# Sums of key blocks on GpSimd for two of four head groups, and norms, halves and first scores at other slots of a hand-written order

## The chip, the cores and the metric

The kernel runs on one core of a Trainium2 chip. A core has five engines with a queue of instructions each: PE (TensorE, matrix products; its weight loads are shown apart as PEld), DVE (VectorE), ACT (ScalarE), POOL (GpSimd) and SP (SyncE, which here issues most DMAs). Each queue is worked in order. Engines wait for one another by semaphores. The metric is the device time in microseconds (us) of one execution; lower is better.

## The reference

One transformer block, 16 sequences of 512 tokens with 512 features, 16 heads of 32, then a mixture of 32 experts (4 for each token) and a shared expert:

```python
x = x + attention(layernorm(x))
x = x + moe(layernorm(x))
# attention, for each sequence and head:
scores = einsum('bsnh,btnh->bnst', k, q) / sqrt(32)
scores = triu(scores) + -10000.0 * tril(ones, k=-1)
attn = softmax(scores, axis=2)
out = einsum('bnkq,bknh->bqnh', attn, v) @ Wo + bo
```

The softmax runs over the keys. Its denominator for a query is the sum of exp(scores) over the keys that are not masked.

## The kernel before

Two parts run one after the other: the sequences (attention, router and shared expert) and then the 32 experts. The change touches the first part alone.

The sequences are worked in 18 turns. Turn i does the projections of sequence i, the attention of sequence i - 1, and the output projection, router and shared expert of sequence i - 2. Turns 0, 1 and 2 and turns 15, 16 and 17 lack some of these; turns 3 to 14 stand in a loop of two turns at a time. A turn has 126 slots (`N_SLOTS`). Each engine walks through the same slots in its own function `turn`, and at each slot issues what the tables at the top of the file (`ST_SLOT`, `S_SLOT` and so on) put there. So the order of each queue is written out by hand, and the tables are the only thing that sets it. A dense product of the projections or the shared expert takes one to four slots on PE. A slot of it is three fp16 matmuls (L172, L173, L174), since each operand is held as a high and a low half.

Heads are worked in four groups of four (`QUARTER`, at slots 0, 30, 60 and 90). For a group, and counted from its first slot:

- PE makes the scores with queries in the partitions (`scores`, L524) in ten fills, f = 0 to 9, of two banks in turn, at the slots of `S_AT`. DVE takes their maxima (`maxima`, L917) one slot later; PE may write fill f only when the maxima of fill f - 2 are read. The first group (0) is that of the next sequence, and its fills lie at slots 85 to 111. `NM_SLOT` follows the last fill by two slots: the maxima are transposed there, and SP places them for the exponentials.
- PE makes the transposed scores, keys in the partitions (`scores_T`, L539), in ten fills at slots 0, 2, ... 18. ACT takes the exponential one slot later (`exp`, L650) and writes `probs`, 1280 columns of f32 for each head: for key block 0 its 512 queries, for the blocks 1, 2 and 3 the 384, 256 and 128 that are not masked (`PCOL` says where each block starts).
- POOL zeroes the triangles on the diagonal (`triangles`, L1033), for two heads each at slots 11 and 20.
- PE forms the product with V (`values`, L548 into `o_ps`) at slot 23 and the product of a matrix of ones with `probs` (`denominators`, L548 into `scores_T`) at slot 25. The latter gives the denominators in f32, 16 matmuls with 32 columns of weights each, the four heads in four column groups of the array.
- DVE transposes and inverts the denominators at slot 26 (`reciprocals`, L931 to L935), normalises at slot 30 (`normalise`, L939), ACT takes the high half at slot 31 (`att_hi`, L656), DVE the low half at slot 35 (`att_lo`, L943).

The other work that the steps below speak of: the statistics of the next sequence are on DVE at slots 82, 84, 86 and 88 (`statistics1`, L697), their scales on POOL two slots later (`scales1`, L1001 to L1006), the norms on ACT at slots 87 to 93 (`norm1`, L628), and the transposes on PE at slots 106, 107, 112 and 113 (L481). The router's selection is a chain of small DVE steps, one at each slot from 73 to 93. The GLU of the shared expert is on ACT (L622) and DVE (L894, L899). From turn 3 on POOL issues one of 16 scatters of router records (L1042) at each third slot from 61 to 106. POOL also subtracts for the low halves of q and k (`qk_lo`, L1025) and adds the output bias to the residual (L1019).

In the trace of a steady turn, slots are recognised by these operations: the product with V of the third group is slot 83, fill 0 of the first scores is slot 85, and the transposed scores f = 3 of the fourth group are slot 96.

Of the kernel before, what the change touches and what calls it, by code (L numbers as in the profile page):

```python
# [11 lines left out]
ALU = mybir.AluOpType  # L12
# [3 lines left out]
P = 128  # L16
BATCH, SEQ, D = 16, 512, 512
# [54 lines left out]
def last_slot(kind, n):  # L72
    at = 0
    for k, m, pieces in GROUPS:
# [5 lines left out]

QUARTER = (0, 30, 60, 90)
FILLS = 10
ST_SLOT = {base + 2 * f: (q, f) for q, base in enumerate(QUARTER) for f in range(FILLS)}

S_AT = {1: range(1, 21, 2), 2: (23, 25, *range(31, 47, 2)), 3: (47, 49, 51, 53, *range(61, 73, 2)),
        0: (85, 91, 94, 97, 100, 103, 105, 107, 109, 111)}
S_SLOT = {slot: (hg, f) for hg, slots in S_AT.items() for f, slot in enumerate(slots)}
EXP_SLOT = {slot + 1: at for slot, at in ST_SLOT.items()}
MAX_SLOT = {slot + 1: at for slot, at in S_SLOT.items()}
NM_SLOT = {slot + 2: hg for slot, (hg, f) in S_SLOT.items() if f == FILLS - 1}  # L90
TRI_SLOT = {base + at: (q, p) for q, base in enumerate(QUARTER) for p, at in enumerate((11, 20))}
PV_SLOT = {base + 23: q for q, base in enumerate(QUARTER)}
DEN_SLOT = {base + 25: q for q, base in enumerate(QUARTER)}
RDEN_SLOT = {base + 26: q for q, base in enumerate(QUARTER)}
ATT_SLOT = {base + 30: q for q, base in enumerate(QUARTER)}
AHI_SLOT = {base + 31: q for q, base in enumerate(QUARTER)}
ALO_SLOT = {base + 35: q for q, base in enumerate(QUARTER)}

S_FILL = tuple(piece for p in range(2) for piece in (
    ((2 * p, 3, 0, 512),), ((2 * p, 0, 0, 128), (2 * p, 2, 128, 384)),  # L100
# [9 lines left out]

LN2_SLOT = {last_slot("out", t) + 4: t for t in range(TT)}
STAT_SLOT = {slot: t for t, slot in enumerate((82, 84, 86, 88))}
LN1_SLOT = {slot + 5: t for slot, t in STAT_SLOT.items()}

ROUTE_FROM = last_slot("router", 0) + 1
DEST_FROM = [last_slot("pos", n) for n in range(2)]
# [170 lines left out]
def sequences(nc, a, c, ps):  # L287
    with ExitStack() as ctx:
# [19 lines left out]

        s_done, s_read, nm_ready = sem("s_done"), sem("s_read"), sem("nm_ready")
        nm_placed = [sem("nm_placed0"), sem("nm_placed1")]  # L310
        st_done, exp_done, tri_done = sem("st_done"), sem("exp_done"), sem("tri_done")
        den_done, den_read, o_done, att_done = sem("den_done"), sem("den_read"), sem("o_done"), sem("att_done")
        aT_hi, aT_ready = sem("aT_hi"), sem("aT_ready")

# [145 lines left out]
        def _(pe):  # L460
# [82 lines left out]
            def columns(bank, loaded):  # L543

                for kt in range(TT):
                    for h in range(GH):
                        n = SEQ - kt * P
                        last = pe.matmul(bank[h * HD:(h + 1) * HD, kt * P:SEQ], loaded(kt, h),  # L548
                                         c["probs"][:, h, PCOL[kt]:PCOL[kt] + n], start=kt == 0, stop=kt == TT - 1)
                return last  # L550

            def denominators(s, hg):

                n = s * HG + hg
                pe.wait_ge(tri_done, (n + 1) * 2)
                pe.wait_ge(exp_done, (n + 1) * FILLS)
                columns(ps["scores_T"][1], lambda kt, h: c["ones"][:, 0:HD]).then_inc(den_done, 1)

            def values(s, par, hg):
                n = s * HG + hg  # L560
# [437 lines left out]
        def _(pool):  # L998
# [28 lines left out]
            def triangles(s, hg, p):  # L1027

                pool.wait_ge(exp_done, (s * HG + hg) * FILLS + (p + 1) * FILLS // 2)
                settle(pool)  # L1030
                for kt in range(TT):
                    blk = c["probs"][:, 2 * p:2 * p + 2, PCOL[kt]:PCOL[kt] + P]
                    last = pool.affine_select(out=blk, in_=blk, compare_op=ALU.is_ge, fill=0.0, base=0,  # L1033
                                              pattern=[[0, 2], [1, P]], channel_multiplier=-1)
                last.then_inc(tri_done, 1)

            def scatter(s, n):
                t, k = divmod(n, TOPK)
                if n == 0:
                    pool.wait_ge(dest_ready, s + 1)  # L1040
                    settle(pool)
                pool.indirect_dma_start(  # L1042
                    out=a["slots"], out_offset=bass.IndirectOffsetOnAxis(ap=c["idx"][:, t, k:k + 1], axis=0),
                    in_=c["rec"][:, t, k, :], in_offset=None, bounds_check=SLOTS - 1,
                    oob_is_err=False).then_inc(slots_scattered, 16)

            def turn(i, par, proj, attn, fin, nxt):
                for slot in range(N_SLOTS):
                    if attn and slot in TRI_SLOT:
                        triangles(i - 1, *TRI_SLOT[slot])  # L1050
                    if proj and slot in QLO_SLOT:
                        qk_lo(i, *QLO_SLOT[slot])
                    if fin and slot in BIAS_SLOT:
                        add_bias(i - 2, BIAS_SLOT[slot])
                    if fin and slot in SCALE2_SLOT:
                        scales2(i - 2, SCALE2_SLOT[slot])
                    if nxt and slot in SCALE1_SLOT:
                        scales1(i + 1, SCALE1_SLOT[slot])
                    if (not isinstance(i, int) or i > 2) and slot in SCATTER_SLOT:
                        scatter(i - 3, SCATTER_SLOT[slot])  # L1060
# [255 lines left out]
def transformer_block(nc, a):  # L1316
    with ExitStack() as ctx:
# [6 lines left out]
        with ExitStack() as first:  # L1324
            def sb(name, shape, dt=F32):
                return first.enter_context(nc.sbuf_tensor(name, shape, dt))
# [18 lines left out]
            c["glu"], c["att"], c["denT"] = sb("glu", [P, 2, 512]), sb("att", [P, SEQ]), sb("denT", [P, SEQ])  # L1345
            c["junk"] = sb("junk", [P, 2, SEQ], F16)
            c["nmax"], c["nmF"], c["nmT"] = sb("nmax", [P, 32]), sb("nmF", [P, 32]), sb("nmT", [P, 2, 32], F16)
            c["rden"] = sb("rden", [P, SEQ // 32])
            c["bqk"] = sb("bqk", [P, 2 * HG])
            c["bvT"], c["bo"], c["maskrow"] = sb("bvT", [P, DK]), sb("bo", [P, D]), sb("maskrow", [P, SEQ], BF16)  # L1350
# [76 lines left out]
```

## Time and profile before

| what | value |
|---|---|
| median of 3 runs | 2513.14 us (2513.05 to 2518.89) |
| profiled execution | 2517.61 us, of which 2515.8 us span |
| mean granted PE clock | 0.966 of full speed |
| PE busy | 2311.3 us, 92% |
| DVE, ACT, POOL busy | 63%, 43%, 44% |
| from 2100 us on | the experts |

The page gives shares over the whole span; a timeline gives single instructions in the order of their start, with the idle time before them on their engine and what ended it.

### The profile page before, as it was taken

Reading aid. Unit: us, or ns where it says so; the run is one execution under the profiler, and the core shown is the slowest. Engines: PE = TensorE matmul, PEld = TensorE weight load, DVE = VectorE, ACT = ScalarE, POOL = GpSimd, SP = SyncE. Lnnn points to the kernel's source line nnn. Section 1 sums busy time; section 2 is a strip of 40 time slices with the busy share of each in tenths; the row PEclk is TensorE's granted clock in tenths of the full one; section 3 lists DMA queues with packets and bytes.
Section 4 is the critical chain, followed back from the end, with each engine's and each line's share of the span. In section 5 each row is a group of like instructions: output and inputs, shape, how many; then the busy total and the mean of one; then the engine's idle time right before and its main releaser. Section 6 shows DMA issues by size and latency. Waiting matters only on the chain. (4 is left out here: it accounts for less than half of the span.)

```text
span 2515.8 us, 48721 instructions
## 1 busy us (share of the span) xinstructions
PE 2311.3 (92%) x15466; PEld 1159.8 (46%) x15466; DVE 1573.3 (63%) x4870; ACT 1083.8 (43%) x1849; POOL 1110.4 (44%) x1622
## 2 busy tenths in 40 slices
PE   3789999999999999999999999999998985999997
PEld 1334444444444444444444444444443443666664
DVE  4355666675766666666666666666666564666664
ACT  3344444444343434343434443434443313666664
POOL 1223244434343434444444444444443354777775
PEclk8889999999999999999999999999998897999999
DMA  4212222222222222222222222222212016888886
GB/s 166 68 43 60 53 69 58 67 55 72 57 66 61 65 67 57 66 69 61 60 61 60 60 60 60 60 60 60 62 41 76 10 55 184 230 233 238 236 234 121
DMA packets 180850, 222.52 MB, mean 88 GB/s; under 512 B 37776, under 2 KB 119792, under 8 KB 180624
## 3 DMA queue, kind: packets, MB, share of 16 engines
q1 hardware_dynamic: 154000, 177.58, 23.7%
q0 software_dynamic: 26624, 42.12, 7.5%
q8 instruction: 118, 1.93, 0.3%
q14 instruction: 108, 0.88, 0.1%
HBM read 112.65 MB, written 56.46 MB: 67 GB/s over the span
## 5 line engine op out<-in xcount | busy, mean ns | idle before, releaser
L917 DVE CUSTOM_DVE_ANT_0 junk<-scores,maskrow 128x512 f16<-128x512 f32 (+3 forms) x1024 | 462.5, 487 | 198.2 <-PE scores L524 130.8
L650 ACT ACTIVATE probs<-scores_T 128x512 f32<-128x512 f32 x640 | 369.6, 598 | 215.8 <-PE scores_T L539 212.9
L1033 POOL TENSOR_SCALAR_AFFINE_SELECT probs<-probs 128x256 f32<-128x256 f32 x512 | 192.6, 413 | 380.8 <-ACT probs L650 379.9
L539 PE MATMUL scores_T<-stack_q,stack_k 97*128 97x512 f16 (+3 forms) x1024 | 251.9, 308 | 53.3 <-ACT probs L650 42.7
L1042 POOL DMA_INDIRECT slots_dram<-rec,idx x256 | 258.8, 1011 | 89.0 <-issue 80.1
L524 PE MATMUL scores<-stack_k,stack_q 96*128 96x512 f16 (+3 forms) x1024 | 253.7, 310 | 44.6 <-DVE nmax L917 41.0
L172 PE MATMUL dense<-xT_hi,wqkv_hi 128*128 128x512 f16 x512 | 196.1, 383 | 1.5 <-DVE xT_lo L888 1.5
L173 PE MATMUL dense<-xT_lo,wqkv_hi 128*128 128x512 f16 x512 | 195.0, 381 | 0.0
L174 PE MATMUL dense<-xT_hi,wqkv_lo 128*128 128x512 f16 x512 | 194.9, 381 | 0.0
L1019 POOL TENSOR_TENSOR xres<-xres,bo 128x512 f32<-128x512 f32 x64 | 81.2, 1268 | 247.3 <-DMA xres<-in_x 247.3
L1159 POOL DMA_INDIRECT out<-ex_y,ex_sidx x96 | 153.3, 1597 | 76.6 <-issue 39.1
L607 ACT ACTIVATE glu<-dense,bqk 128x512 f32<-128x512 f32 x128 | 88.0, 687 | 218.4 <-PE dense L174 211.8
L524 PEld LDWEIGHTS scores<-stack_k,stack_q 96*128 96x128 f16 x1024 | 95.4, 100 | 183.9 <-DVE nmax L917 93.1
L539 PEld LDWEIGHTS scores_T<-stack_q,stack_k 97*128 97x128 f16 x1024 | 98.6, 100 | 174.1 <-ACT probs L650 55.7
L1025 POOL TENSOR_TENSOR split_q<-glu,split_q 128x512 f16<-128x512 f32 x64 | 74.3, 1161 | 217.2 <-ACT split_q L607 217.2
L548 PE MATMUL o_ps<-probs,v 128*32 128x512 f32 (+3 forms) x2048 | 156.5, 447 | 8.1 <-POOL probs L1033 5.5
L548 PE MATMUL scores_T<-probs,ones 128*32 128x512 f32 (+3 forms) x2048 | 151.2, 436 | 0.0
L1137 POOL DMA_INDIRECT ex_xg<-x2n_dram,ex_gidx x96 | 118.6, 1235 | 47.1 <-POOL ex_gidx L1132 27.6
L888 DVE SCALAR_TENSOR_TENSOR xT_lo<-dense,xT_hi 128x512 f16<-128x512 f32 x128 | 87.9, 689 | 78.9 <-ACT xT_hi L598 78.9
L1001 POOL TENSOR_SCALAR mv<-mv 128x1 f32<-128x1 f32 x128 | 29.5, 231 | 230.4 <-DVE mv L699 226.7
L931 DVE STREAM_TRANSPOSE denT<-scores_T 128x512 f32<-128x512 f32 x64 | 45.8, 716 | 136.1 <-PE scores_T L548 136.1
L598 ACT ACTIVATE xT_hi<-dense 128x512 f16<-128x512 f32 x128 | 74.4, 598 | 106.9 <-PE dense L481 91.5
(229 smaller groups left out, 5486.2 us busy)
## 6 DMA issues: line engine op xcount, KB each, us to landing
stack_q<-split_q SPq DMA_DIRECT2D x384, 64.0 KB, 2.0
stack_k<-split_k SPq DMA_DIRECT2D x384, 64.0 KB, 2.3
out<-xres SPq DMA_DIRECT2D x67, 256.0 KB, 3.1
xres<-in_x SPq DMA_DIRECT2D x64, 256.0 KB, 2.9
x2n_dram<-x2n SPq DMA_DIRECT2D x16, 1024.0 KB
ex_raw_wg<-in_W_gate SPq DMA_DIRECT2D x32, 512.0 KB, 4.1
ex_raw_wu<-in_W_up SPq DMA_DIRECT2D x32, 512.0 KB, 5.1
ex_raw_wd<-in_W_down SPq DMA_DIRECT2D x32, 512.0 KB, 8.6
```

The source lines that it names most:

```text
L172: pe.matmul(out, w[0], x[0], start=start, stop=False)
L173: pe.matmul(out, w[0], x[1], start=False, stop=False)
L174: return pe.matmul(out, w[1], x[0], start=False, stop=stop)
L524: last = pe.matmul(bank[:, at:at + cols], c["stack_q"][0:SROWS, hg, h, qt * P:(qt + 1) * P], c["stack_k"][0:SROWS, hg, h, 0:cols], start=T ...
L539: last = pe.matmul(bank[:, at:at + cols], c["stack_k"][0:SROWS + 1, hg, h, kt * P:(kt + 1) * P], c["stack_q"][0:SROWS + 1, hg, h, kt * P:k ...
L548: last = pe.matmul(bank[h * HD:(h + 1) * HD, kt * P:SEQ], loaded(kt, h), c["probs"][:, h, PCOL[kt]:PCOL[kt] + n], start=kt == 0, stop=kt = ...
L650: act.activation(to, at, ACT.Exp, scale=SCALE / (QS * QS)).then_inc(exp_done, 1)
L917: last = dve.tensor_tensor_reduce(out=c["junk"][:, f % 2, at:at + cols], in0=ps["scores"][f % 2][:, at:at + cols], in1=c["maskrow"][:, SEQ ...
L1033: last = pool.affine_select(out=blk, in_=blk, compare_op=ALU.is_ge, fill=0.0, base=0, pattern=[[0, 2], [1, P]], channel_multiplier=-1)
L1042: pool.indirect_dma_start(out=a["slots"], out_offset=bass.IndirectOffsetOnAxis(ap=c["idx"][:, t, k:k + 1], axis=0), in_=c["rec"][:, t, k, ...
L1137: pool.indirect_dma_start(out=e_["xg"][q][0:r, ch, :], out_offset=None, in_=a["x2n"], in_offset=bass.IndirectOffsetOnAxis(ap=e_["gidx"][q] ...
L1159: pool.indirect_dma_start(out=a["out"], out_offset=bass.IndirectOffsetOnAxis(ap=e_["sidx"][q][0:r, ch:ch + 1], axis=0), in_=e_["y"][q][0:r ...
```

## The change

For the head groups 1 and 2 (slots 30 and 60) POOL adds the key blocks 1, 2 and 3 of `probs` into a new tile `psum` of 384 columns a head, in three adds for two heads each (768, 512 and 256 elements in a partition) directly behind the triangles of the same heads. For these groups the product with ones then has 128 columns of block 0 and 384 columns of `psum` a head, in 8 matmuls where there were 16, with a wait for the adds. It moves from slot 25 to 27 of its group, the reciprocals from 26 to 28. The groups 0 and 3 keep the old form.

In all groups the high half moves from slot 31 to 33 (group 3: from 121 to 122) and the low half from 35 to 36 (group 3: from 125 to 124). The norms of the next sequence move from slots 87, 89, 91 and 93 to 94, 96, 98 and 100. The fills of the first scores move as the first hunk shows.

```diff
+SUMMED = (1, 2)
-        0: (85, 91, 94, 97, 100, 103, 105, 107, 109, 111)}
+        0: (85, 91, 93, 96, 99, 101, 104, 107, 110, 113)}
-DEN_SLOT = {base + 25: q for q, base in enumerate(QUARTER)}
-RDEN_SLOT = {base + 26: q for q, base in enumerate(QUARTER)}
+DEN_SLOT = {base + 25 + 2 * (q in SUMMED): q for q, base in enumerate(QUARTER)}
+RDEN_SLOT = {base + 26 + 2 * (q in SUMMED): q for q, base in enumerate(QUARTER)}
-AHI_SLOT = {base + 31: q for q, base in enumerate(QUARTER)}
-ALO_SLOT = {base + 35: q for q, base in enumerate(QUARTER)}
+AHI_SLOT = {slot: q for q, slot in enumerate((33, 63, 93, 122))}
+ALO_SLOT = {slot: q for q, slot in enumerate((36, 66, 96, 124))}
-LN1_SLOT = {slot + 5: t for slot, t in STAT_SLOT.items()}
+LN1_SLOT = {slot + 12: t for slot, t in STAT_SLOT.items()}
@@ PE: denominators
-                columns(ps["scores_T"][1], lambda kt, h: c["ones"][:, 0:HD]).then_inc(den_done, 1)
+                if hg not in SUMMED:
+                    columns(ps["scores_T"][1], lambda kt, h: c["ones"][:, 0:HD]).then_inc(den_done, 1)
+                    return
+                pe.wait_ge(summed, (s * len(SUMMED) + SUMMED.index(hg) + 1) * 2 * 3)
+                for at, x in ((0, c["probs"][:, :, 0:P]), (P, c["psum"])):
+                    for h in range(GH):
+                        last = pe.matmul(ps["scores_T"][1][h * HD:(h + 1) * HD, at:at + x.shape[2]], c["ones"][:, 0:HD], x[:, h, :], start=True, stop=True)
+                last.then_inc(den_done, 1)
@@ POOL
+            def block_sums(s, hg, p):
+                n = (s * len(SUMMED) + SUMMED.index(hg)) * 2 + p
+                pool.wait_ge(tri_done, (s * HG + hg) * 2 + p + 1)
+                if p == 0:
+                    need(pool, den_done, s * HG + hg)
+                heads = slice(2 * p, 2 * p + 2)
+                to, of = c["psum"], c["probs"]
+                pool.tensor_tensor(to[:, heads, :], of[:, heads, P:SEQ], of[:, heads, PCOL[1]:PCOL[1] + 384], ALU.add).then_inc(summed, 1)
+                pool.wait_ge(summed, n * 3 + 1)
+                pool.tensor_tensor(to[:, heads, P:384], to[:, heads, P:384], of[:, heads, PCOL[2]:PCOL[2] + 256], ALU.add).then_inc(summed, 1)
+                pool.wait_ge(summed, n * 3 + 2)
+                pool.tensor_tensor(to[:, heads, 256:384], to[:, heads, 256:384], of[:, heads, PCOL[3]:PCOL[3] + P], ALU.add).then_inc(summed, 1)
@@ POOL: turn
                     if attn and slot in TRI_SLOT:
                         triangles(i - 1, *TRI_SLOT[slot])
+                        if TRI_SLOT[slot][0] in SUMMED:
+                            block_sums(i - 1, *TRI_SLOT[slot])
@@ memory
+            c["psum"] = sb("psum", [P, GH, SEQ - P])
```

## Rows read from the trace of the kernel before

**Rows 1.** Page, part 1: busy time of each engine, share of the span, instructions.
```profile
PE 2311.3 (92%) x15466; PEld 1159.8 (46%) x15466; DVE 1573.3 (63%) x4870; ACT 1083.8 (43%) x1849; POOL 1110.4 (44%) x1622
```
**Rows 2.** Timeline of PE, slots 83 to 100: start, duration, line, form, [idle before].
```profile
1014.57 2.36 PE L548 MATMUL o_ps<-probs,v 128*32 128x512 f32 x32
...
1018.17 0.38 PE L524 MATMUL scores<-stack_k,stack_q 96*128 96x512 f16 x1
...
1031.05 0.39 PE L539 MATMUL scores_T<-stack_q,stack_k 97*128 97x384 f16 x2 [2.52 <-ACT probs L650]
...
1032.63 0.63 PE L174 MATMUL dense<-xT_hi,suT_lo 128*128 128x512 f16 x1
...
1035.99 0.38 PE L539 MATMUL scores_T<-stack_q,stack_k 97*128 97x512 f16 x1
```
**Rows 3.** Timeline of PE, slot 96 two turns later.
```profile
1276.17 0.39 PE L539 MATMUL scores_T<-stack_q,stack_k 97*128 97x384 f16 x2 [2.52 <-ACT probs L650]
```
**Rows 4.** Waits of PE: who for whom, us in total, times, longest.
```profile
PE scores_T L539 <- ACT probs L650: 42.7, 22, 3.9
PE scores L524 <- DVE nmax L917: 41.0, 44, 3.9
```
**Rows 5.** Timeline of PE: slot 71 of one turn, slots 111 to 115 of another.
```profile
1128.86 0.39 PE L524 MATMUL scores<-stack_k,stack_q 96*128 96x256 f16 x2 [0.65 <-DVE nmax L917]
...
1045.84 0.39 PE L524 MATMUL scores<-stack_k,stack_q 96*128 96x256 f16 x2 [0.72 <-DVE nmax L917]
...
1050.78 2.36 PE L548 MATMUL scores_T<-probs,ones 128*32 128x512 f32 x32
1053.07 0.39 PE L172 MATMUL dense<-sdT_hi,hT_hi 128*128 128x512 f16 x1
```
**Rows 6.** Timeline of ACT, same turn as rows 2, slots 89 to 93.
```profile
1027.22 0.81 ACT L628 ACTIVATE x2n<-x2n,mv 128x512 f32<-128x512 f32 x1 [2.18 <-POOL mv L1006]
1029.39 0.63 ACT L656 ACTIVATE aT_hi<-att 128x512 f16<-128x512 f32 x1 [1.36 <-DVE att L939]
...
1030.40 0.59 ACT L650 ACTIVATE probs<-scores_T 128x512 f32<-128x512 f32 x1
```
**Rows 7.** Timeline of DVE, same turn, slots 84 to 92.
```profile
1019.00 0.69 DVE L894 SCALAR_TENSOR_TENSOR glu<-glu,dense 128x512 f32<-128x512 f32 x1 [2.48 <-ACT glu L622]
...
1023.64 0.69 DVE L917 CUSTOM_DVE_ANT_0 junk<-scores,maskrow 128x512 f16<-128x512 f32 x1 [0.37 <-DVE att L935]
...
1030.86 0.08 DVE L917 DVE_READ_ACCUMULATOR2_ANT nmax<- 128x1 f32 x1
```
**Rows 8.** Page, part 5: additions and subtractions of POOL, busy and mean ns.
```profile
L1019 POOL TENSOR_TENSOR xres<-xres,bo 128x512 f32<-128x512 f32 x64 | 81.2, 1268 | 247.3 <-DMA xres<-in_x 247.3
...
L1025 POOL TENSOR_TENSOR split_k<-glu,split_k 128x512 f16<-128x512 f32 x64 | 74.2, 1160 | 60.6 <-ACT split_k L607 60.6
```
**Rows 9.** Timeline of POOL, second head group, slot 50.
```profile
1109.26 1.49 POOL L1033 TENSOR_SCALAR_AFFINE_SELECT probs<-probs 128x256 f32<-128x256 f32 x4 [2.90 <-ACT probs L650]
```
**Rows 10.** Timeline of PE, second head group, slots 55 and 57.
```profile
1114.50 2.36 PE L548 MATMUL scores_T<-probs,ones 128*32 128x512 f32 x32
...
1118.10 0.60 PE L492 MATMUL dense<-ident,x2n 128*128 128x128 f32 x4
```
**Rows 11.** Timeline of POOL, same turn as rows 2, third head group, slots 71 to 80.
```profile
1006.05 1.49 POOL L1033 TENSOR_SCALAR_AFFINE_SELECT probs<-probs 128x256 f32<-128x256 f32 x4 [11.64 <-ACT probs L650]
1007.70 0.99 POOL L1042 DMA_INDIRECT slots_dram<-rec,idx  x1 [0.16 <-issue]
...
1010.27 0.97 POOL L1042 DMA_INDIRECT slots_dram<-rec,idx  x1 [0.30 <-issue]
1012.40 1.54 POOL L1033 TENSOR_SCALAR_AFFINE_SELECT probs<-probs 128x256 f32<-128x256 f32 x4 [1.15 <-ACT probs L650]
```
**Rows 12.** Timeline of PE, turn 1: two waits and what follows them.
```profile
168.46 4.05 PE L548 MATMUL o_ps<-probs,v 128*32 128x512 f32 x32 [2.34 <-POOL probs L1033]
...
178.37 0.39 PE L524 MATMUL scores<-stack_k,stack_q 96*128 96x512 f16 x1 [1.79 <-DVE nmax L917]
```

More of the change, by code:

```diff
@@ L310, in sequences @@
         nm_placed = [sem("nm_placed0"), sem("nm_placed1")]
-        st_done, exp_done, tri_done = sem("st_done"), sem("exp_done"), sem("tri_done")
+        st_done, exp_done, tri_done, summed = sem("st_done"), sem("exp_done"), sem("tri_done"), sem("summed")
         den_done, den_read, o_done, att_done = sem("den_done"), sem("den_read"), sem("o_done"), sem("att_done")
```

## Prediction

> **What bounds the kernel now.** I read the page's busy times first, then the waits of PE, then one sequence turn of PE's timeline and, beside it, what VectorE, ScalarE and GpSimd do in the same microseconds. PE is busy in 92% of the span [rows 1], so every stage is PE's unless a wait shows otherwise. The 126 slots of a turn are worked in about 122.6 us: the same wait stands at 1031.05 and at 1276.17, two turns later [rows 2, 3], and (1276.17 - 1031.05) / 2 = 122.6. In a steady turn PE waits three times: 0.65 us at slot 71 (1128.86), about 2.5 to 2.9 us at slot 96, and 0.72 us at slot 111 [rows 2, 4, 5]. The long wait costs more than its length. From 1.6 us after it, matmuls of 512 columns take 0.63 us instead of 0.38, and follow each other at 0.43 instead of 0.22, until 1035.99 [rows 2]: ten of them at 0.21 extra, some 1.65 us. So PE's own work is the bound in all of the turn but slots 84 to 97.
>
> That stretch has another bound behind it. ScalarE reaches the exp for which PE waits only at 1030.40, held first by a norm that waits for GpSimd, then by a high half that waits for VectorE [rows 6]. But VectorE is itself full: from 1019.00 (GLU of slot 84, 0.8 us after PE ended that slot at 1018.17) it works without a pause, bar 0.37 us, until the maxima of score fill 1 are read at 1030.94 [rows 2, 7]. That is 11.9 us of VectorE work per turn, and PE may not write score fill 3 before it is done. This is the point to hold on to: moving norms and halves takes ScalarE's wait away, not VectorE's.
>
> **The change, part by part.**
>
> Shorter product with ones. Today the 16 matmuls of one head group start at 1050.78 and the next work at 1053.07: 2.3 us for 1280 columns a head, four heads beside each other [rows 5]. The new form has 128 + 384 = 512 columns a head. By columns alone 2.3 x 512/1280 = 0.92 us; I add 0.1 for starting and take 1.0, so 1.3 us saved, for two of four groups in 16 turns. If it were all PE's bound, 32 x 1.3 = 42 us.
>
> The three adds on GpSimd. One call adds 2 x 384, 2 x 256 and 2 x 128 elements, 1536 together. The nearest row is the add of 512 f32 elements at 1268 ns [rows 8]. Whatever part of it is fixed, three adds with 512 elements in the mean cost 3 x 1.268 = 3.8 us; with two hand-overs, at the 0.16 us that lie between the triangles and the next work of this engine [rows 11], I take 4.1 us. The lower bound is 3 x 1.16 = 3.5 by the subtraction row [rows 8]; the upper is 4.6, with 0.2 us for each of three hand-overs and 5% on each add. Per turn there are four calls, 16 us, which GpSimd has idle in sum (it is busy 44% [rows 1]); only their place matters.
>
> The Trainium skill (GPSIMD Engine Reference, section 3.1) puts a two-input add at about 2.6 cycles an element at 1.2 GHz, and calls the engine the wrong choice for plain elementwise work. An estimate by that page is 1536 x 2.6 / 1.2 = 3.3 us before dispatch, where the row gives 3.8; by it the stall below would be 0.5 us shorter. The trace agrees within the dispatch that the page leaves open.
>
> Second head group (slots 30 to 59). Its second triangle call starts at 1109.26 and ends at 1110.75 [rows 9]; the adds then end at 1114.9. The product, moved from slot 55 to 57, comes 1.3 us (two slots) after 1114.50, at 1115.8 [rows 10]. So it does not wait, with 0.9 us to spare; even the upper bound of the adds, 0.5 us more, leaves 0.4. Behind the first call only a subtraction for k is late (1100.5 to 1104), read by nobody for several slots. The reciprocals follow two slots later and PE is not held by them. Gain 1.3 us a turn; the wait at slot 71 moves with PE and stays 0.65.
>
> Third head group (slots 60 to 89). Here GpSimd's queue matters. After the first triangle call (1006.05 to 1007.54) it issues three scatters of slots 73, 76 and 79, ending at 1011.24, idles 1.15 us, and runs the second call from 1012.40 to 1013.94; PE needs it for the product with V at 1014.57 [rows 2, 11]. The spare time is 1.15 + 0.63 = 1.8 us. The first call's adds are put in front of the three scatters: 4.1 - 1.8 = 2.3 us too late, so PE stalls 2.3 us at slot 83, where it never waited. Bounds: 3.5 - 1.8 = 1.7 and 4.6 - 1.8 = 2.8. A stall of 2.34 us in front of this same product was followed by 4.05 us for it instead of 2.36; after 1.79 us the next matmul took its 0.39 [rows 12]. So I add the 1.65 us at the lower clock: PE ends slot 84 by 4.0 us late. The second call's adds end near 1021.2, before PE comes to the product at slot 87 near 1024: no wait there.
>
> What is late next: the 11.9 us of VectorE begin with the GLU of slot 84 and no step among them is moved out before the maxima of slot 92 (reciprocals go from 86 to 88, the normalisation stays at 90). So score fill 3, now at slot 96, goes out at 1031.05 + 4.0. PE waits there again, longer than now (its own work from slot 84 to there is some 9 us), with the same loss of clock afterwards as today. The 1.3 us saved at slot 87 vanish in that wait. In exchange, one score fill (0.2 us) now lies before the wait's end instead of after it.
>
> Norms, high and low halves. The norms at slots 94 to 100 instead of 87 to 93, the high half at 93 instead of 91: ScalarE no longer stands before the exps of slots 91 and 93. Four norms and three exps around slots 94 to 100 are some 5.5 us in 7 us of PE work, which fits. The gain is nil because of VectorE. The transposes that need the norms are at 106 and later.
>
> First scores. The fills at 93, 96, 99, 101, 104, 107, 110, 113 leave VectorE more time at the end: the wait of 0.72 us at slot 111 [rows 5] should go, 0.7 us gained. The maxima are sent two slots later, but are needed at slot 0 of the next turn; I see some 3 us left there, so nothing.
>
> **The sum.** Per steady turn: -1.3 (second group) + 4.0 (stall and clock, carried on by VectorE) - 0.2 - 0.7 = +1.8 us. Scatters, and so this queue, are in turns 3 to 16; 13 of these (3 to 15) have all parts: 13 x 1.8 = +23 us. Turn 2 has no scatters: -2.2. Turn 1 has a stall at the same product already [rows 12], which gets some 2 to 3 us longer and is partly paid by the shorter products; turn 16 has no first scores and loses the stall of 4.0 less 2.6. I take the three together as nil, with 3 us to either side. The stage of the experts is untouched. The profiled execution is 2515.8 us of span and 1.8 around it, 2517.6, so it would become 2541; it lies 4.5 above the median of the runs, 2513.1, and against the median the forecast is 2536.
>
> **The rivals.**
>
> Rival 1, GpSimd is early enough (faster). If the adds cost 1.8 us or less per call, no stall arises at slot 83. Then VectorE still binds slot 96, and a turn gains 1.3 + 0.2 + 0.7 = 2.2 us: 14 x 2.2 = 31, about 2482. Against it: 1.8 us for 1536 elements would be twice the rate of [rows 8]. A smaller form of it: stall of 1.7 us without loss of clock ([rows 12] shows none after 1.79), so -1.3 + 1.7 - 0.9 = -0.5 a turn, 2507, within or just beyond what counts as no change.
>
> Rival 2, the stall comes but is absorbed (faster). If VectorE isn't the bound at slot 96 (because its work shrinks while PE stands, or ScalarE alone made the wait), then today's 2.7 + 1.65 us go, the 4.0 take their place, and both products gain: -1.3 - 1.3 - 0.7 - 0.3 = -3.6 a turn, 2463 to 2470. For it: the wait in [rows 2, 4] is put down to ScalarE. Against: VectorE's maxima end 0.11 us before PE resumes [rows 2, 7].
>
> Rival 3, the two stalls together cost more clock (slower). They stand some 14 us apart; if the second low stretch is twice as long, 1.65 us more a turn, or if the later maxima delay the residual loads and so GpSimd in the first group by 0.5 us: 13 x 2 = +26, about 2560.
>
> Rival 4, the change doesn't act: the stall and the gains cancel, 2513.
>
> **How the numbers follow.** Forecast 0.50; rival 1 full 0.12, its smaller form 0.10; rival 2 0.10; rival 3 0.14; rival 4 0.04. Three tenths of a per cent, 7.5 us, is what a measurement of this kernel can tell from no change. Faster: 0.12 (rival 1) + 0.10 (rival 2) + 0.03 of the smaller form = 0.25. Same: the rest of the small form, rival 4, and 0.02 of the forecast's low side = 0.13. Slower 0.62. The forecast's own range is 2524 to 2550 (stall 1.9 to 2.8). For 8 in 10 I go from 2475 to 2558; that leaves out rival 2 and part of rival 3. The cases of both signs lie in it.
>
> **What would show it.** Right: PE's product with V at slot 83 waits 2.3 us for the triangles of the third group; the second triangle call starts directly behind a scatter; score fill 3 waits for VectorE's maxima; the short products take 1.0 us; the wait at 111 is gone; a turn lasts 124.4 us. The three adds show 1.8, 1.27 and 0.7 us. Wrong: no wait at slot 83, or a wait at slot 96 that is gone while VectorE is idle there, or turns below 121 us.

## The result, and the profile after

The changed kernel takes 2551.82 us (median of 4 runs, 2549.71 to 2555.69) beside 2514.64 us for the kernel before in the same comparison: a ratio of 1.0147, interval 1.0128 to 1.0166. It is slower by 37 us, where 23 us were forecast (2536 us): inside the range given for 8 in 10 (2475 to 2558), just above the forecast's own range (2524 to 2550). Its profiled execution took 2550.47 us, 2548.7 of them span. That is 32.9 us of span more than before, and 32.4 of these lie in the twelve steady turns 3 to 14.

The page of after, part 1, answers to [rows 1]: GpSimd is busy 53% of the span, and TensorE is busy for fewer microseconds in a longer span, at the lower share of 90%.

```profile
PE 2292.3 (90%) x14954; PEld 1145.2 (45%) x14954; DVE 1604.5 (63%) x4870; ACT 1083.4 (43%) x1849; POOL 1357.0 (53%) x1814
```

The waits of PE in after (who for whom, us in total, times, longest), beside [rows 4]:

```profile
PE scores L526 <- DVE nmax L926: 82.1, 72, 3.5
PE o_ps L550 <- POOL probs L1042: 40.2, 22, 5.0
...
PE scores_T L541 <- ACT probs L659: 15.5, 21, 1.3
```

Waits for the maxima have doubled (they were 41.0), those for the exps have fallen from 42.7, and the product with V waits 40 us in all for GpSimd's triangles. The timeline of PE in one steady turn of after shows where; start, us, instruction, and in brackets the idle time before it:

```profile
1124.48 0.39 PE L526 MATMUL scores<-stack_k,stack_q 96*128 96x512 f16 x1 [0.53 <-DVE nmax L926]
...
1127.13 0.39 PE L526 MATMUL scores<-stack_k,stack_q 96*128 96x128 f16 x2 [0.74 <-DVE nmax L926]
...
1147.50 0.39 PE L526 MATMUL scores<-stack_k,stack_q 96*128 96x256 f16 x2 [0.65 <-DVE nmax L926]
...
1158.03 2.36 PE L550 MATMUL o_ps<-probs,v 128*32 128x512 f32 x32 [2.18 <-POOL probs L1042]
...
1163.24 0.43 PE L565 MATMUL scores_T<-probs,ones 128*32 128x128 f32 x8
1163.48 0.83 PE L565 MATMUL scores_T<-psum,ones 128*32 128x384 f32 x8
...
1171.65 0.39 PE L541 MATMUL scores_T<-stack_q,stack_k 97*128 97x384 f16 x2 [0.95 <-ACT probs L659]
...
1174.46 0.61 PE L526 MATMUL scores<-stack_k,stack_q 96*128 96x128 f16 x2 [2.41 <-DVE nmax L926]
```

The third row from the top is the old wait of slot 71 [rows 5]. The fourth is the forecast stall of slot 83: 2.18 us. The last two are slot 96: a short wait for an exp, then 2.41 us for the maxima of score fill 1. The first two, at slots 43 and 45, are new and were not forecast. GpSimd in the same turn, around slots 71 to 80:

```profile
1147.26 1.49 POOL L1042 TENSOR_SCALAR_AFFINE_SELECT probs<-probs 128x256 f32<-128x256 f32 x4 [7.08 <-ACT probs L659]
1148.83 1.81 POOL L1054 TENSOR_TENSOR psum<-probs 128x768 f32<-128x768 f32 x1
1150.72 1.27 POOL L1056 TENSOR_TENSOR psum<-psum,probs 128x512 f32<-128x512 f32 x1
1152.07 0.73 POOL L1058 TENSOR_TENSOR psum<-psum,probs 128x256 f32<-128x256 f32 x1
1152.94 0.99 POOL L1065 DMA_INDIRECT slots_dram<-rec,idx  x1 [0.15 <-issue]
...
1155.52 0.97 POOL L1065 DMA_INDIRECT slots_dram<-rec,idx  x1 [0.31 <-issue]
1156.49 1.49 POOL L1042 TENSOR_SCALAR_AFFINE_SELECT probs<-probs 128x256 f32<-128x256 f32 x4
```

Triangles, three adds, three scatters, triangles. The second triangle call starts at 1156.49, where the third scatter ends; in [rows 11] 1.15 us of idle time lay between them.

For all kernels below I cut the turns 3 to 14 into four stretches by PE's marks: slot 0 to the product with V of slot 53, from there to the router (slot 69), to the product with V of slot 83, and to the next slot 0. Means of 12 turns, in us (differences between kernels are then free of what happens outside the steady turns). The last four rows come from other chips than the rest, as told further down:

| kernel | 0 to 53 | 53 to 69 | 69 to 83 | 83 to 0 | turn |
|---|---|---|---|---|---|
| before | 50.06 | 16.44 | 9.90 | 45.91 | 122.31 |
| after | 51.78 | 15.19 | 12.16 | 45.88 | 125.01 |
| e1, slots only | 50.65 | 16.44 | 9.91 | 43.67 | 120.66 |
| e2, adds of group 2 only | 51.78 | 15.19 | 9.91 | 44.09 | 120.97 |
| e3, adds of group 3 only | 50.47 | 16.44 | 12.16 | 45.42 | 124.49 |
| e4, scatters earlier | 51.80 | 15.19 | 9.91 | 44.84 | 121.73 |
| e5, destination steps later | 50.92 | 15.19 | 12.16 | 45.46 | 123.73 |
| e6, e4 and e5 | 51.01 | 15.19 | 9.91 | 45.01 | 121.12 |
| e7, e6 and late statistics | 50.98 | 15.19 | 9.91 | 43.36 | 119.44 |
| e8, e1 and late statistics | 50.13 | 16.44 | 9.90 | 44.18 | 120.65 |
| e9, e8 and all scatters early | 50.42 | 21.01 | 9.88 | 42.31 | 123.62 |
| e10, e9, adds of group 2, steps later | 51.34 | 20.59 | 10.03 | 42.27 | 124.23 |
| e11, kernel of e9 | 50.49 | 22.19 | 9.87 | 42.50 | 125.05 |
| e12, kernel of e7 | 50.86 | 20.98 | 9.99 | 43.64 | 125.47 |

Here group 2 is the second head group (slots 30 to 59, number 1 in the code) and group 3 the third (number 2).

### The profile page after: what moved, and what is told of

It reads as the page before. It is cut to its first block and busy times, and to the rows that moved or that the text cites. A ratio compares the mean times of both kernels' runs of the same rounds, so it can differ in the third digit from the quotient of the medians.

```text
span 2548.7 us, 48087 instructions
## 1 busy us (share of the span) xinstructions
PE 2292.3 (90%) x14954; PEld 1145.2 (45%) x14954; DVE 1604.5 (63%) x4870; ACT 1083.4 (43%) x1849; POOL 1357.0 (53%) x1814
## 5 line engine op out<-in xcount | busy, mean ns | idle before, releaser
L1065 POOL DMA_INDIRECT slots_dram<-rec,idx x256 | 264.5, 1033 | 86.2 <-issue 78.4
L550 PE MATMUL o_ps<-probs,v 128*32 128x512 f32 (+3 forms) x2048 | 163.6, 463 | 43.1 <-POOL probs L1042 40.2
L631 ACT ACTIVATE glu<-dense 128x512 f32<-128x512 f32 x64 | 38.2, 597 | 233.7 <-PE dense L176 191.5
L550 PEld LDWEIGHTS o_ps<-probs,v 128*32 128x32 f32 x2048 | 63.3, 115 | 148.2 <-issue 85.0
L1054 POOL TENSOR_TENSOR psum<-probs 128x768 f32<-128x768 f32 x64 | 116.1, 1814 | 5.3
```

Of the source, the lines that this page charges most:

```text
L1054: pool.tensor_tensor(to[:, heads, :], of[:, heads, P:SEQ], of[:, heads, PCOL[1]:PCOL[1] + 384], ALU.add).then_inc(summed, 1)
L1065: pool.indirect_dma_start(out=a["slots"], out_offset=bass.IndirectOffsetOnAxis(ap=c["idx"][:, t, k:k + 1], axis=0), in_=c["rec"][:, t, k, ...
```

## The experiments

**The change taken apart: e1, e2, e3.** `SUMMED` lists the head groups whose keys GpSimd adds; everything else stays as in the changed kernel.

```diff
-SUMMED = (1, 2)
+SUMMED = ()
```

This is e1; e2 has (1,) there and e3 has (2,).

> The changed kernel with no group summed: all four products with ones in the old form at slot 25, no adds on GpSimd, but norms, halves and first scores at their new slots. Theory: VectorE binds score fill 3 at slot 96, so the moved norms and halves gain nothing; only the wait of 0.72 us at slot 111 and one score fill go, 0.9 us a turn, so 2500 to 2512 us against 2514.6 before, and PE's wait at slot 96 is put down to VectorE's maxima, 3 us or more a turn. Rival (ScalarE alone made the wait at slot 96): the wait is gone, some 4 us a turn, about 2460. Rival (the moved slots are what costs): above 2530.

> The changed kernel with sums and short product for the second head group alone. Theory: no stall at slot 83, since the adds in front of three scatters belong to the third group. The product gains 1.3 us a turn, but GpSimd's adds hold up VectorE's steps of slot 43 and PE waits 0.5 and 0.7 us for maxima, so nothing is left of it: within 4 us of the kernel with moved slots alone. Rival (those two waits come from the low half at slot 36 or another moved slot, not from the adds): they stand in the kernel with moved slots alone as well, and this one is 18 us faster than that.

> The changed kernel with sums and short product for the third head group alone. Theory: the stall at slot 83 (2.2 us, in half of the turns with a low clock behind it) is here and carries nearly the whole loss: 2545 to 2556, as the changed kernel; no waits at slots 43 and 45. Rival (the loss is spread over both groups): near 2530.

Measured: e1 2493.99 us, ratio 0.9916 (0.9899 to 0.9933); e2 2501.56, 0.9947 (0.9927 to 0.9967); e3 2547.02, 1.0118 (1.0100 to 1.0135). So the moved slots alone are a gain of 0.8%, and both sets of adds take from it: 7.6 us for group 2, 53 us for group 3. e3 came as expected. e1 is 6 us faster than the 2500 to 2512 expected, and e2 lies 7.6 us above e1, where at most 4 were expected. The two waits of slots 43 and 45 stand in e2 and not in e1 or e3, so they come with the adds of group 2 and not with a moved slot.

In e1 the wait of slot 96 is still there, now put down to VectorE, and the wait of 0.72 us at slot 111 is gone. Timeline of PE, e1, two turns in a row:

```profile
1019.63 0.39 PE L526 MATMUL scores<-stack_k,stack_q 96*128 96x128 f16 x2 [2.26 <-DVE nmax L926]
...
1051.41 0.39 PE L526 MATMUL scores<-stack_k,stack_q 96*128 96x512 f16 x1 [0.83 <-DVE nmax L926]
...
1140.54 0.39 PE L526 MATMUL scores<-stack_k,stack_q 96*128 96x128 f16 x2 [2.42 <-DVE nmax L926]
```

The wait is 2.26 and 2.42 us in alternate turns, where the kernel before has 2.52 and 2.89. After the first of them the granted clock stays at its upper level (2.4 GHz): the table of windows of e1 (window, its length, busy us of PE, PEld, DVE, ACT, POOL with counts, granted clock, DMA share, GB/s) has 1.00 behind the wait of 1019.63, and 0.50 (1.2 GHz) behind that of 1140.54.

```profile
1021.00:1023.00 2.00, 2.00 (x13) 1.11 (x12) 2.00 (x8) 2.00 (x5) 1.70 (x2) 1.00 0.03 4
...
1142.00:1144.00 2.00, 2.00 (x7) 0.91 (x6) 2.00 (x8) 2.00 (x4) 1.70 (x2) 0.50 0.04 8
```

Counted over the twelve steady turns, the clock was low behind the wait of slot 96 in ten turns of the kernel before and in three of e1. The mean granted clock over turns 3 to 14 is 0.99 in before, 1.00 in e1, 0.97 in after.

The first stretch of e1 is 0.59 us longer in the mean. Most turns have nothing of it. Three turns have a wait of up to 0.87 us (0.83 in the row at 1051.41) for the maxima of the first scores, which the change reads later. Two of these three also wait 2.10 and 1.59 us for GpSimd's triangles, ahead of the first product with V. What makes these late stays open. PE of e1, the second of the two:

```profile
827.16 2.36 PE L550 MATMUL o_ps<-probs,v 128*32 128x512 f32 x32 [1.59 <-POOL probs L1042]
```

In e2 the product of slot 57 is short and the stretch from slot 53 to 69 falls by 1.25 us (forecast: 1.3), but the stretch ahead of it grows by 1.13 us against e1: the waits of slots 43 and 45. These are VectorE's, and VectorE itself had been slowed. Two of its lines, grouped over 300 to 1800 us of after (busy us, mean ns of one):

```profile
L850 DVE TENSOR_TENSOR denT<-sc,top 128x128 f32<-128x128 f32 x48 | 29.0, 661 | 0.4
L935 DVE CAST nmT<-nmF 128x32 f16<-128x32 f32 x48 | 18.4, 382 | 1.7
```

the same lines in e2, where only group 2 has adds:

```profile
L850 DVE TENSOR_TENSOR denT<-sc,top 128x128 f32<-128x128 f32 x48 | 29.0, 662 | 0.4
...
L935 DVE CAST nmT<-nmF 128x32 f16<-128x32 f32 x50 | 9.3, 187 | 1.7
```

and in e3, where only group 3 has them:

```profile
L935 DVE CAST nmT<-nmF 128x32 f16<-128x32 f32 x48 | 18.4, 382 | 1.7
L850 DVE TENSOR_TENSOR denT<-sc,top 128x128 f32<-128x128 f32 x48 | 10.8, 287 | 0.4
```

Same instructions, same data. The mean of L850 more than doubles where the adds of group 2 run beside it, and the mean of the CAST doubles with the adds of group 3: one of its four instances in a turn takes 0.98 us in place of 0.18 to 0.21, in every steady turn of after. One turn of after shows how. VectorE:

```profile
1121.32 2.42 DVE L850 TENSOR_TENSOR denT<-sc,top 128x128 f32<-128x128 f32 x4
...
1149.69 0.98 DVE L935 CAST nmT<-nmF 128x32 f16<-128x32 f32 x1
```

and GpSimd beside the first of them:

```profile
1120.22 1.27 POOL L1056 TENSOR_TENSOR psum<-psum,probs 128x512 f32<-128x512 f32 x1
1121.57 0.85 POOL L1058 TENSOR_TENSOR psum<-psum,probs 128x256 f32<-128x256 f32 x1
1122.39 1.20 POOL L1034 TENSOR_TENSOR split_k<-glu,split_k 128x512 f16<-128x512 f32 x1
```

The four pieces of L850 take 0.90 us in the kernel before and 2.42 us here, beside two of the adds and the subtraction for k that now comes behind them. The CAST, 0.18 us where it is alone, ends at 1150.67, 0.03 us after the add L1054 of the GpSimd rows further up (1148.83 + 1.81 = 1150.64). By these times it stood until that add was over.

SBUF is the memory on the chip that holds the tiles. The Trainium skill says this beforehand: GpSimd shares its SBUF interfaces with VectorE, and collides with VectorE instructions in a two-port mode or with two SBUF inputs (GPSIMD Engine Reference, section 8, Key points); whichever starts first holds the pair for its whole instruction and the other one blocks (SBUF — State Buffer, section "SBUF: two separate sides"). The traces agree for L850, which has two inputs in SBUF, and for the end of the CAST.

**The stall of slot 83: e4.** Seven scatters that stood at every third slot from 61 to 79 are issued in slots 61 to 70, ahead of the first triangle call of group 3, so that only the adds lie between its two triangle calls.

```diff
-SCATTER_SLOT = {slot: n for n, slot in enumerate(range(61, 109, 3))}
+SCATTER_SLOT = {slot: n for n, slot in enumerate((61, 62, 64, 65, 67, 68, 70, *range(82, 109, 3)))}
```

> The changed kernel with three scatters moved from slots 73, 76 and 79 to 62, 65 and 68, where GpSimd idles 7 us. Theory: the adds before the second triangle call then end in time, the stall at slot 83 is gone, and so are 2.2 us and its low clock, 3 us a turn: 2505 to 2516. The wait at slot 96 for VectorE's maxima stays, and is longer than in the changed kernel, since PE comes there earlier. Rival (the adds are late whatever stands between): the stall stays and the time is within 5 us of 2552. Rival (VectorE is not the bound behind it): the wait at slot 96 shrinks too and the time falls below 2490.

Measured: 2506.54 us, 0.9965 (0.9950 to 0.9979). The stretch 69 to 83 is back at 9.91 us from 12.16, and 83 to 0 falls by 1.04 more. So the stall of slot 83 was a matter of GpSimd's order, not of its load: 45 us of the kernel's time, with the clock it cost. One part of the expectation missed: the wait of slot 96 did not grow, it stayed at 0.9 us for an exp and 2.42 us for the maxima. TensorE comes earlier by the length of the stall, but so does VectorE's chain, which starts with slot 84. Together the two waits are 1.0 us more than the 2.34 us of e1, so that the 1.3 us saved by the short product at slot 87 mostly go into this wait, and behind it the clock was low in ten of twelve turns, against three in e1.

**VectorE's slowed steps: e5, e6.** The four steps of the destination reckoning (which works out where the router's records go) that hold L850 and its successors come three slots later, behind most of the adds of group 2. e5 does this to the changed kernel, e6 to e4.

```diff
+DEST_STEP = {at: n for n, at in enumerate((0, 1, 2, 6, 7, 8, 9))}
...
-                        if 0 <= slot - DEST_FROM[m] < len(DESTINATIONS):
-                            DESTINATIONS[slot - DEST_FROM[m]](s, bank)
+                        if slot - DEST_FROM[m] in DEST_STEP:
+                            DESTINATIONS[DEST_STEP[slot - DEST_FROM[m]]](s, bank)
```

> The changed kernel with the last four steps of the record chain on VectorE (slots 43 to 46) at slots 46 to 49, so that they no longer run beside the adds of GpSimd for the second group. Theory: these steps have two inputs in memory and stand still while GpSimd adds, which is why four of 0.3 us took 2.4 us; moved, they take about 1.1 us together again, the waits of 0.54 and 0.73 us at slots 43 and 45 go, and slots 0 to 53 take 50.7 us instead of 51.8: 13 to 17 us less than the changed kernel, about 2536. Rival (VectorE is late there by the moved low half or by its own work): the waits stay, or move to slots 46 to 49 in the same sum, and the time is within 5 us of 2552.

> Both repairs, the record steps later and three scatters earlier. Theory: the two causes are independent and add: 2506 of the kernel with early scatters alone less 14 is 2492. Rival: they overlap, 2500 to 2508.

Measured: e5 2535.28 us, 1.0070 (1.0053 to 1.0087); e6 2495.73, 0.9918 (0.9902 to 0.9935). Moving only VectorE's steps, with GpSimd's work untouched, takes the ratio from 1.0147 to 1.0070 for the changed kernel, and from 0.9965 to 0.9918 for e4. e5 came as expected; e6 lies 4 us above the 2492 expected and below the 2500 to 2508 of its rival. The first stretch falls by 0.86 us (51.78 to 50.92). The waits of 0.54 and 0.73 us are gone, but a new one of 0.84 us for maxima stands a few slots later. Part of the steps still lies beside adds, as the grouped line of e5 shows (one line further down in that kernel):

```profile
L851 DVE TENSOR_TENSOR denT<-sc,top 128x128 f32<-128x128 f32 x48 | 22.3, 524 | 0.0
```

**The wait of slot 96: e7, e8.** The statistics of tiles 2 and 3 and their norms come later, which takes VectorE's work out of the chain that slot 96 waits for. e7 does it to e6, e8 to e1.

```diff
-STAT_SLOT = {slot: t for t, slot in enumerate((82, 84, 86, 88))}
-LN1_SLOT = {slot + 12: t for slot, t in STAT_SLOT.items()}
+STAT_SLOT = {slot: t for t, slot in enumerate((82, 84, 94, 97))}
+LN1_SLOT = {slot: t for t, slot in enumerate((94, 96, 101, 104))}
```

> As the one before, and the statistics of tiles 2 and 3 of the next sequence go from slots 86 and 88 to 94 and 97, their norms to 101 and 104. Theory (VectorE's work between slots 84 and 92 is the bound at slot 96): the chain ahead of the maxima of slot 92 is shorter by 1.9 us, and the wait for them shrinks from 2.4 (and 0.9 for an exp) by as much: 20 to 25 us less, about 2470. Rival (the wait has another cause, or the statistics are missed at slot 94 instead): less than 8 us.

> The kernel with moved slots alone (no sums), and the same two statistics later. Theory: the wait of 2.4 us at slot 96 falls to 0.5 to 0.7, 1.8 us a turn, so 24 us less than 2494, about 2470. Rival: no change.

Measured: e7 2471.93 us, 0.9825 (0.9808 to 0.9841), as expected; e8 2489.17, 0.9893 (0.9876 to 0.9909), a miss: 5 us less than e1 instead of 24, and not even these in the steady turns (120.65 and 120.66 us a turn). In e8 the wait of slot 96 did shrink, to 1.11 and 0.73 us in alternate turns, but the last product with V of the turn waits instead. PE of e8:

```profile
1133.27 0.39 PE L526 MATMUL scores<-stack_k,stack_q 96*128 96x128 f16 x2 [1.11 <-DVE nmax L926]
...
1148.94 1.39 PE L550 MATMUL o_ps<-probs,v 128*32 128x512 f32 x12 [1.69 <-POOL probs L1042]
```

and GpSimd of e8 ahead of it:

```profile
1136.43 0.46 POOL L1010 TENSOR_SCALAR mv<-mv 128x1 f32<-128x1 f32 x1 [6.35 <-DVE mv L708]
...
1144.86 1.27 POOL L1065 DMA_INDIRECT slots_dram<-rec,idx  x1 [0.17 <-issue]
1146.44 0.97 POOL L1065 DMA_INDIRECT slots_dram<-rec,idx  x1 [0.30 <-issue]
1147.41 1.48 POOL L1042 TENSOR_SCALAR_AFFINE_SELECT probs<-probs 128x256 f32<-128x256 f32 x4
```

GpSimd stands 6.35 us for the late statistics, the scatters of slots 94 to 106 pile up behind it, and the second triangle call comes too late. e7 has the same pile, but TensorE comes to its product later after slot 96 (15.2 us after the wait's end, in e8 14.0 without the stall), behind a wait of 1.63 us that the lower clock follows, and finds it ready. In eleven of the twelve steady turns of e7 it is so. In the one turn where e7's clock stayed up, the product waits as in e8. PE of e7:

```profile
542.86 2.36 PE L551 MATMUL o_ps<-probs,v 128*32 128x512 f32 x32 [1.70 <-POOL probs L1043]
```

The gain of e8 was eaten by a wait that had no room before: in e7 the lower clock left it that room.

**The pile removed, and what came of it: e9, e10, e11, e12.** All sixteen scatters stand ahead of the late statistics; e9 is e8 with this, e10 is e7 with this and the adds of group 2 alone.

```diff
+SCATTER_SLOT = {slot: n for n, slot in enumerate((61, 62, 64, 65, 67, 68, 70, 72, 74, 76, 82, 84, 86, 88, 90, 92))}
```

> The slots of the changed kernel without any adds and with the statistics of tiles 2 and 3 late (as e8), and in addition all sixteen scatters queued before the late statistics (slots 61 to 76 and 82 to 92), none behind them. In the run e8 the wait at slot 96 had shrunk from 2.42 to 1.11 us, but GpSimd stood 6.35 us for VectorE's mean and variance, five scatters piled up behind it, the triangles came late and the product of slot 113 waited 1.69 us. Theory (this pile of scatters is what took e8's gain): the 1.69 us goes, in 13 turns 22 us, about 2467 us. Rival (the third and fourth statistics themselves make GpSimd late, not the scatters): the wait at slot 113 stays and the time is e8's, 2485 to 2493 us. Second rival: the fourth group's product comes at its old time but TensorE's clock falls after the wait at slot 96 again, about 2480 us.

> As e9, with GpSimd's adds for the second head group alone and the destination steps 3 to 6 at slots 46 to 49, as e5. In e7 the stretch from slot 0 to the router takes 66.17 us, in e8 66.57 us, so that with its neighbour held off the adds, the short product is worth 0.4 us a turn, 5 us in all. Theory: 5 us below e9, about 2462 us. Rival (the adds cost more than their product saves even so, since GpSimd's later triangles and halves wait for them): at or above e9, 2467 to 2475 us.

Measured: e9 2549.50 us, 1.0048 (1.0031 to 1.0065); e10 2558.04, 1.0075 (1.0058 to 1.0091), both against 2537.29 for the kernel before, which had been at 2514 to 2517 in every comparison so far. Both are misses, by 82 and 96 us, and e10 lies 8.5 us above e9 instead of 5 below. The part under test did what the theory said: the wait of slot 113 is gone and the last stretch of e9 is 42.31 us after 44.18 in e8. But the stretch 53 to 69 is 21.01 us instead of 16.44, with PE idle for reasons that the profile doesn't show. Timeline of PE, e9:

```profile
1001.77 0.49 PE L494 MATMUL dense<-ident,x2n 128*128 128x128 f32 x3 [0.73 <-issue]
1003.45 0.38 PE L174 MATMUL dense<-wqkv_hi,xT_hi 128*128 128x512 f16 x1 [1.19 <-issue]
1004.88 0.38 PE L174 MATMUL dense<-wqkv_hi,xT_hi 128*128 128x512 f16 x1 [0.62 <-issue]
```

Do the ten close scatters do this, or the chip of that comparison? Two more runs ask: the kernel of e9 and that of e7 again.

> The kernel of e9 once more, beside that of e7, whose rows are known. In e9 the wait at slot 113 went, as its theory said (slot 83 to the next slot 0 fell from 44.18 us in e8 to 42.31), but the stretch from the product of slot 53 to the router grew from 16.44 to 21.01 us, in which TensorE stood for nothing that the profile shows (0.73, 1.19 and 0.62 us in one turn), while GpSimd issued seven scatters in a row, and the kernel before was 22 us above its other medians in that comparison. Theory (the ten scatters of slots 61 to 76, close together, bring this stall): the stretch stays near 21 us here and e11 is slower than e7 by 70 us or more, at 2530 to 2550 us. Rival (the stall belongs to the chip of that comparison and not to the kernel): if the kernel before is near 2515 us here, the stretch is 16.4 us and e11 near 2467 us; if it is near 2537 us, e12 has the stall as well.

> The kernel of e7 once more, with seven scatters in slots 61 to 70 instead of ten in 61 to 76. Theory (ten close scatters bring the stall, seven do not): its stretch from the product of slot 53 to the router is 15.2 us as in e7, and its time 0.9825 of the kernel before on whichever chip. Rival (the chip): where the kernel before is near 2537 us, the stretch is longer than 17 us here too and the ratio is nearer to one.

Measured: e11 2568.12 us (2530 to 2550 expected), 1.0103 (1.0075 to 1.0131); e12 2574.61, 1.0137 (1.0115 to 1.0159), against 2541.44 for the kernel before. So the kernel of e7, unchanged, is 1.75% faster than before in one comparison and 1.4% slower in another. Its stretches here are 50.86, 20.98, 9.99 and 43.64 us: all within 0.3 us of e7 but the second, 15.19 there. In that stretch of e12 GpSimd issues seven scatters in a row, from 1001.56 to 1010.33, and ACT stands from 1005.2, PE from 1008.3 and DVE from 1008.8 on. The rows with which ACT, DVE and PE go on ("remote" and "issue" name no instruction of this core that was waited for; PE waits for ACT):

```profile
1012.30 0.60 ACT L660 ACTIVATE probs<-scores_T 128x512 f32<-128x512 f32 x1 [7.11 <-remote]
```
```profile
1012.53 0.42 DVE L927 CUSTOM_DVE_ANT_0 junk<-scores,maskrow 128x256 f16<-128x256 f32 x1 [3.77 <-remote]
```
```profile
1012.95 0.61 PE L542 MATMUL scores_T<-stack_q,stack_k 97*128 97x512 f16 x1 [4.65 <-ACT probs L660]
```

The twelve experiments ran on four chips. On two of them (e1 to e4, and e5 to e8) the kernel before was at 2516; on two others (e9 and e10, e11 and e12) at 2537 to 2541, and there every one of the four runs has this stretch 4.6 to 5.8 us longer. The theory that ten close scatters bring the stall and seven do not is out: e11, with ten, is 6 us faster than e12, with seven. The rival of e11 holds in that it takes such a chip: e7 has the same seven scatters and no such stall. (Each comparison had a chip of its own, so "the chip" stands here for all that differed between them.)

The stretch is 5.8 us a turn longer in e12 than in e7, 70 of the 103 us between them in the twelve steady turns. Another 13 lie at the end of the sequences, from the last product of the router to the first transposes of the experts' inputs: 77.5 us in e12 (2080.77 to 2158.27), 64.3 in e7 (1992.88 to 2057.21). There GpSimd issues fourteen scatters in a row, from 2085.40 to 2102.99, and VectorE of e12 stands from 2098.2 to 2105.36:

```profile
2105.36 0.69 DVE L909 SCALAR_TENSOR_TENSOR glu<-dense,glu 128x512 f32<-128x512 f32 x1 [7.13 <-remote]
```

This row of scatters at the end stands in the kernel before too, which loses 21 to 25 us on those chips against the 103 us of this kernel. That it takes close scatters besides the chip is thus likely, but it is not shown: no kernel with scatters three slots apart was traced on such a chip. Neither is it known what the changed kernel takes there, nor what is slow on those chips. What e4 and e6 to e8 say is thus said for chips of the first kind only; differences inside one comparison stand.

What is left of the adds, by an estimate from the table: with the second stretch of e8, e9 would take 123.62 - 21.01 + 16.44 = 119.1 us a turn with no adds at all, and e7, the fastest kernel here, took 119.4 with both sets. By this estimate the adds gain nothing once slots, statistics and scatters lie well; no run shows it on one chip.

## Why the prediction was right, and where it was off

The direction and the mechanism of the loss were right; the sum was 0.9 us a turn too small (forecast +1.8, measured 125.01 - 122.31 = +2.7). That it came so near is in part luck: the second group was taken 1.6 us too well and the moved slots 0.75 us too badly, and the two partly cancel. Term by term, in us a turn:

| term | forecast | measured | from |
|---|---|---|---|
| moved slots | -0.9 | -1.65 | e1 less before |
| adds of group 3, stall and clock | +4.0 | +3.83 | e3 less e1 |
| adds of group 2 | -1.3 | +0.31 | e2 less e1 |
| the parts together | | +0.21 | rest |

- **Durations.** The adds take 1.81, 1.27 and 0.73 us, 4.1 a call with the hand-overs: as forecast. The short product takes 1.0 us from 1163.24 to the next work: as forecast. The three together are 3.8 us; the estimate by the rate that the Trainium skill gives (GPSIMD Engine Reference, section 3.1) was 3.3, so that the measurement decides for the row of before.
- **Stall of slot 83.** 2.18 us of the forecast 2.3, in front of the product it was forecast for, with the second triangle call directly behind a scatter. The low clock after it was taken as certain from one row; in after it is seen in five of the twelve steady turns (the product takes 4.06 us at 1030.82, 2.36 at 1158.03), in e3 in four. So the stall costs less than 4.0 in itself; e3 comes to 3.83 with more low clock later in the turn: behind the wait of slot 96 the clock was low in all twelve turns of e3, against three of e1.
- **Carried on by VectorE.** From the GLU of slot 84 at 1162.46 to the wait's end at 1174.46 lie 12.0 us, forecast 11.9, and PE waits there 0.95 and 2.41 us. Rival 2, that the stall is absorbed, is out: e4 takes the stall away and a turn falls by 3.3 us. The cost of a low stretch, 1.65 us, was right, but its working was not: eight matmuls at 0.21 us extra give it, not ten.
- **Moved slots.** This term was mis-sized. The wait of slot 111 went, as said, but the first stretch of the next turn grew by 0.59 us in the mean, where the prediction counted nothing: a third of it waits for the later maxima, half of it waits for GpSimd's triangles. And the wait of slot 96 fell from 2.52 and 2.89 us to 2.26 and 2.42, and the clock was low behind it in three turns of twelve instead of ten; the prediction left it at its old length and clock. The last stretch lost 2.24 us. By an estimate 0.7 of them are the wait of slot 111, 0.4 the shorter wait, and 1.0 the clock (seven turns of twelve at 1.65 us).
- **Second head group.** The step that failed. "So it does not wait" was right for the product, but the adds were costed only by who waits for GpSimd, not by what VectorE does in the same microseconds. They lengthened L850 and others, and VectorE, which is close to PE there, passed it on: +1.13 us before slot 53. Another 0.42 us stand in the last stretch, where the clock was low in five turns of e2 and three of e1. e5 shows the first part by the opposite move, of VectorE's steps and nothing else.
- **Rival 3** (more low clock, 2560 us) is partly what happened: the mean granted clock of the steady turns is 0.97 in after, 0.99 in before. In five of the twelve turns of after the low stretch behind the second wait lasted 5.8 to 6.1 us, in the others 2.8 to 3.4.

## What to carry over

When work is handed to GpSimd, look up not only what stands behind it in its own queue but what VectorE does at that time: two-input and casting steps beside it took twice their time and more here, and a VectorE that was just early enough is then late. A batch of work that nobody waits for soon (here the scatters), placed between two calls that another engine waits for, delays the second by its whole length; moving it ahead of them cost nothing on the chips where it was first tried. And a gain that rests on one chip is to be measured on another before it is believed: here the best version won 1.75% on one chip and lost 1.4% on another.

## What the runs showed of the hardware

- VectorE beside GpSimd's adds: 128x128 steps with two inputs from 0.29 to 0.66 us in the mean, a CAST of 128x32 from 0.19 to 0.38 in the mean, since one in four took 0.98; in the turn shown it ended 0.03 us after the add.
- The clock: of waits of 2.2 to 2.9 us at one and the same place some were followed by 1.2 GHz, mostly for 2.8 to 3.5 us, and some were not (1.00 and 0.50 behind waits of 2.26 and 2.42 us in e1). A stall of 2.18 us was followed by either. A wait of 1.63 us was followed by it in eleven of twelve turns of e7, waits of 1.68 to 1.70 us at another slot in none of e8. So the length of the wait alone does not tell.
- Chips differ, and by kernel: the kernel before by 1% between the comparisons (2516 and 2537 to 2541 us), the kernel of e7 by 4% (2471.93 and 2574.61), 70 of the 103 us in one stretch of the steady turns and 13 at the end of the sequences.
